# Eight transformer layers on one core: the attention gelu of half 0 placed ahead of half 1's second affine step on the scalar engine

## The reference: what is computed

```python
residual = x
Q = fmap(x @ Wq[i] + bq[i])          # fmap(t) = elu(t) + 1
K = fmap(x @ Wk[i] + bk[i])
value = x @ Wv[i] + bv[i]
KV = jnp.einsum('nsh,nsh->nh', K, value)
Ksum = jnp.sum(K, axis=1)
Z = 1.0 / (Q * Ksum[:, None, :] + EPS_ATTN)
V = Q * KV[:, None, :] * Z
attn_out = gelu(V @ Wo[i] + bo[i])
x = _ln(attn_out + residual, ln1_s[i], ln1_b[i])
residual = x
h = gelu(x @ W1[i] + b1[i])
ff_out = gelu(h @ W2[i] + b2[i])
x = _ln(ff_out + residual, ln2_s[i], ln2_b[i])
```

## Time and profile before

| | us |
|---|---|
| median of 3 runs | 715.82 |
| lowest and highest of the 3 | 714.5 and 719.45 |
| the profiled execution, its time | 718.21 |
| the profiled execution, its span | 716.4 |
| PE busy in the span | 633.6 (88%) |
| DVE busy | 432.8 (60%) |
| ACT busy | 318.1 (44%) |
| mean granted PE clock | 0.946 of full speed |

### The profile page before, as it was taken

One profiled execution on the slowest core, in us unless ns is written; L12 is line 12 of the kernel. 1 busy time (PEld: TensorE's weight loads), 2 busy tenths in 40 slices (PEclk: granted clock), 3 DMA queues, 4 the chain that ended last, 5 costly groups with the idle time before them and its releaser, 6 DMA issues.

```text
span 716.4 us, 9508 instructions
## 1 busy us (share of the span) xinstructions
PE 633.6 (88%) x3301; PEld 432.7 (60%) x3301; DVE 432.8 (60%) x1023; ACT 318.1 (44%) x504; POOL 114.4 (16%) x93
## 2 busy tenths in 40 slices
PE   9986899899999898888888898888876988999996
PEld 4755585787777364555555554545455866555595
DVE  5479503347758757666666666575765588643444
ACT  4035202234444556565555656574633434344341
POOL 0030130003230011110111111102032146200000
PEclk9599967989999999999999999999998999999997
DMA  3011388100000501000010101010000000000000
GB/s 86 25 44 46 95 255 175 29 1 1 0 1 1 146 1 44 2 21 25 0 44 0 44 0 44 0 44 1 0 1 0 1 1 0 1 0 1 0 1 30
DMA packets 43726, 21.79 MB, mean 30 GB/s; under 512 B 14627, under 2 KB 40799, under 8 KB 43692
## 3 DMA queue, kind: packets, MB, share of 16 engines
q1 hardware_dynamic: 43692, 21.33, 11.3%
HBM read 20.73 MB, written 0.52 MB: 30 GB/s over the span
## 4 chain that ended last, share of the span: by engine, by line
PE 44%; issue 29%; DVE 19%; POOL 5%; ACT 3%; POOLq 0%; DVEq 0%
PE ps L1515 6%; PE ps L1498 6%; POOL rstd L493 5%; PE ps L1702 5%; PE ps L1720 4%; PE ps L1249 3%; DVE zr L1053 2%; PE ps L1726 2%; DVE z L1012 2%; PE ps L1295 2%; PE ps L1376 2%; PE ps L1582 1%; PE ps L1389 1%; DVE xn L841 1%; PE ps L1416 1%
## 5 line engine op out<-in xcount | busy, mean ns | idle before, releaser
L493 POOL TENSOR_TENSOR rstd<-rv,minus_half 128x4 f32<-128x4 f32 x34 | 47.3, 1392 | 312.0 <-DVE rv L830 312.0
L660 ACT ACTIVATE zr<-ps 128x512 fp32r<-128x512 f32 x96 | 57.5, 599 | 80.0 <-PE ps L1498 76.0
L1053 DVE SCALAR_TENSOR_TENSOR zr<-ps,zr 128x512 fp32r<-128x512 f32 x96 | 63.7, 689 | 47.9 <-ACT zr L660 47.6
L1582 PE MATMUL ps<-cf,wl 128*128 128x512 f32 x128 | 68.5, 640 | 6.9 <-ACT cf L568 6.9
L1588 PEld LDWEIGHTS ps<-wl,z 128*128 128x128 f32 x512 | 64.0, 192 | 17.5 <-ACT z L722 8.7
L815 DVE TENSOR_TENSOR yt<-ps,z 128x512 f32<-128x512 f32 x32 | 22.1, 692 | 80.2 <-ACT z L727 42.4
L1588 PE MATMUL ps<-wl,z 128*128 128x128 f32 x512 | 68.4, 276 | 0.0
L1515 PE MATMUL ps<-zr 128*128 128x512 f32 x192 | 60.8, 398 | 7.8 <-DVE zr L1053 7.8
L1249 PE MATMUL ps<-filler 128*128 128x512 bf16 x246 | 62.9, 401 | 1.2 <-POOL filler L481 0.9
L1498 PE MATMUL ps<-zr 128*128 128x512 f32 x192 | 61.5, 402 | 1.4 <-DVE zr L994 1.4
L1206 DVE SCALAR_TENSOR_TENSOR z<-z,kc 128x512 f32<-128x512 f32 x48 | 34.6, 751 | 46.0 <-ACT z L775 44.2
(11 more groups left out here) (255 smaller groups left out, 1120.9 us busy)
## 6 DMA issues: line engine op xcount, KB each, us to landing
wl<-in_L_attn_W SPq DMA_DIRECT2D x16, 256.0 KB
big<-in_L_cond_weight SPq DMA_DIRECT2D x32, 64.0 KB, 1.8
arena<-in_L_cond_expert_wi SPq DMA_DIRECT2D x1, 1024.0 KB, 6.6
arena<-in_L_cond_expert_wo SPq DMA_DIRECT2D x4, 256.0 KB, 7.5
big<-in_L_ffn_q_w SPq DMA_DIRECT2D x2, 512.0 KB, 5.2
big<-in_L_ffn_k_w SPq DMA_DIRECT2D x2, 512.0 KB, 7.4
tree_v<-in_L_ffn_v_w SPq DMA_DIRECT2D x2, 512.0 KB, 7.4
arena<-in_L_cond_share_wi SPq DMA_DIRECT2D x1, 768.0 KB, 6.6
```

Source lines behind the costliest of these rows:

```text
L493: nc.gpsimd.tensor_tensor(rstd[:, half, :], rv[:, half, :], minus_half[:, :], ALU.pow).then_inc(S_["rstd"], 1)
L660: nc.scalar.activation(hidden_part(h, n, 0), ps[h][:, n % 2, :], ACT.Relu).then_inc(S_[k + "_hi"], 1)
L1053: V.scalar_tensor_tensor(hidden_part(h, n, 1), ps[h][:, n % 2, :], 0.0, hidden_part(h, n, 0), ALU.max, ALU.subtract).then_inc(S_[k + "_lo" ...
L1582: T.matmul(ps[h][:, FFN_BANK[c], :], wl[s][:, 4 * D + c * P:4 * D + (c + 1) * P], cf[:, h], start=True, stop=True).then_inc(S_["f_w1"], 1)
```

## The change

In ACT's `layer`, the call `gelu_o(l, 0)` moves from behind `affine(l - 1, 1, 1 - s, 1)` to ahead of it. In the first layer, which has no such affine step, nothing changes. No other engine's list changes.

```diff
             def layer(l, s, first=False):
                 feature_maps(l, 0, s)
                 ratio(l, 0)
+                gelu_o(l, 0)
                 if not first:
                     affine(l - 1, 1, 1 - s, 1)
-                gelu_o(l, 0)
                 feature_maps(l, 1, s)
                 affine(l, 0, s, 0)
                 ratio(l, 1)
```

## The result

| | before | after |
|---|---|---|
| median, four runs of each (us) | 717.06 (714.5 to 719.45) | 705.21 (703.01 to 707.69) |
| profiled execution, time and span | 718.21, 716.4 | 707.69, 705.8 |
| mean granted PE clock | 0.946 | 0.952 |

The ratio is 0.9843, with a 95% interval from 0.9812 to 0.9874: 1.6% faster. The prediction was 705.6 us and a span of 706.2. Two runs of one later kernel (the kernel before without fillers, 733.41 and 734.68 us) are over 1.5% slower than its fastest and enter no ratio.

A forecast was written before the change was run, and what follows sets the result against it. PE leads, and in each layer its wait for L841, behind the late gelu, ends last. 6.9 us from seven layers plus 3.3 from the clock make 10.2: 715.82 to 705.6 us, range 702.5 to 710.6.

The forecast's parts named there:

- The gelu's place: On ACT in layers 1 to 7: gelu L711 starts 1.11 us earlier, right behind attn_out; affine step L568 0.06 late.
- The chain behind it: DVE from L815 through half 1's queries L1092 to scaling L841 can move 1.11 us earlier; queries have 0.16 to spare.
- What is late next: PE's fillers ahead of the transposes then bound the layer; transposes end 0.98 us earlier per layer, between 0.82 and 1.11.
- The overlap of 0.16: PE's next instruction starts 0.16 us before the modelled end of the one before; without overlap the gain is 0.82.
- Seven layers: The change affects layers 1 to 7, each 0.98 us shorter: 6.9 us together, 5.7 to 7.8 by the ends.
- The clock: Two layers at 1.2 GHz instead of 2.4 cost 1.65 us each; both falls go, 3.3 us, between 0 and 5.0.
- the idle of 0.71 us: PE's wait for scaling L841 ahead of the layer's transposes, before both clock falls; the change takes it out.
- Its rival of more falls: Clock falls in more layers, 1.65 us each; six or seven hit layers lose, all seven give 717.1 us; chance 0.04.
- Its sign of no low clock up to 530 us: In the profile after, no low PE clock between 280 and 530 us; a layer of 37.7 us would refute the clock term.
- The parts that I took as unchanged: Time ahead of and behind the eight attention layers; the change sits only in the layers, about 236 to 535 us.
- The table load: ACT's load L687 runs after the affine step, 1.28 us from the trace; a skill's 2.66 would make the sum about 0.

The follow-up runs named there:

- the affine step was made 0.52 late: Changed kernel plus an unread 128x512 copy on ACT between gelu and affine step in layers 1 to 7; 711.79 us, ratio 0.9912 to before.
- seven fillers: Changed kernel with seven instead of four filler matmuls on PE ahead of the transposes of half 0's first norm; 711.27 us, ratio 0.9924 to before.
- one filler less: Changed kernel with three instead of four filler matmuls on PE ahead of the transposes of half 0's first norm; 707.33 us, ratio 0.9836 to before.
- before, seven fillers: Kernel before with seven instead of four filler matmuls on PE ahead of the transposes of half 0's first norm; 714.21 us, ratio 0.9949 to before.

## Why the prediction was right

**The number is closer than the reasoning.** The forecast change was 10.2 us, the medians differ by 11.85. The forecast started from a median of before of 715.82, which a fourth run moved to 717.06. The two errors nearly cancel, and that 705.6 lies 0.4 from 705.21 is luck; the terms are what can be checked.

**The gelu's place.** Forecast: the gelu 1.11 earlier, and the affine step 0.06 late. Shown: L815 waits 1.28 instead of 2.38, 1.10 less, and PE waits 0.05 longer for the affine step.

**The chain behind it.** Forecast: it moves as a whole, because the queries have 0.16 to spare. Shown: 4.55 from gelu to L841 as before, and, of the runs made, the queries waited only when the affine step was made 0.52 late.

**What is late next.** Forecast: PE's fillers, so that 0.98 of the 1.11 is kept. Shown: period 36.03 for 37.03, so 1.00; seven fillers cost all of their time and one filler less brought 0.11. Had I bound PE's next start by the modelled end of the fillers, it would have been 0.82. The overlap of 0.16, read from one pair of rows, decided that.

**Seven layers.** Forecast 6.9. Shown: the two profiles without a low clock in any layer give it directly: 295.31 (before, seven fillers) less 288.34 (after) is 6.97.

**The clock.** Forecast: both falls go, 3.3. Shown: 3.40 between before and before with seven fillers. The two terms must add up to the 10.37 of the layers' part, since both are taken over the same profile; the check on them is the single layers, where the periods differ by 1.00 and the two hit layers by 1.65 and 1.67 more. That the idle of 0.71 us matters is shown by filling it (ratio 0.9949, all of the interval below 1) and by taking all of its fillers away (1.0066, all of it above 1). Which layers are hit is not settled; nor is why, without fillers, 0.43 and 0.87 us of idle left seven layers untouched. In nine profiles with the gelu ahead everywhere, none of 63 layers with the new order had a low clock; of 25 with the old order (7 each in the two profiles of before and in that without fillers, 4 in that with the gelu ahead in three layers) seven had one, and of 7 with the old order and seven fillers none. The Trainium skill (TensorE: Matmul & The Clock Gate, "A second HAM failure mode: psum-queue depth-cycling") has short idles between groups of matmuls behind such falls, and the filled one agrees: no low clock in its seven layers. The prediction put every fall at 1.65 us, which was right for these two only: elsewhere one cost 1.5 or 3.2 to 3.3. Its rival of more falls has a slip: four more are 4 x 1.65 = 6.6, less than 6.9, so six hit layers would not have made the kernel slower. Its sign of no low clock up to 530 us missed the fall at 528.3, ahead of the last transposes.

**The parts that I took as unchanged** were not, by chance: 1.08 less ahead of the layers and 0.85 more behind. They nearly cancel. Such differences, and layer 0, where the clock may fall in either kernel, are of the size of the 5 us by which runs of one kernel spread; that they are that spread was not tested.

**The table load.** The row (1.28 and the next activation at once) was right and the 2.66 of the Trainium skill (ScalarE: Activation LUTs, "What ACT_TABLE_LOAD costs") would have been wrong here: L687 starts at 352.43, L696 at 353.73, 1.30 behind it. That section of the Trainium skill splits its figure into a load of about 1.28 us and a drain of about 1.38 us. The trace agrees with the first, 1.28, and shows no time for the second.

## What to carry to other kernels

On an engine that runs its list in order, put first what is ready first. Look at who posts the two semaphores: here PE posted the gelu's semaphore 0.43 us before the affine step's, and the reverse order cost 1.1 us on the longer path to save 0.06 on the shorter. Then ask what is late next, and by how much; of 1.1 us here PE's own list left 1.0.

Where the tensor engine idles for less than a microsecond at a time, look at the granted clock layer by layer before summing up waits: here a third of the gain in the layers was clock (3.4 of 10.4 us in the profiles), and three more unused matmuls per layer in the same gap bought about that third alone.

## What the hardware showed that I had not expected

- Fillers that nobody waits for are worth time: without four of them per layer the kernel before is 0.7% slower (0.3 to 1.1%) with no instruction held up, and with three more it is 0.5% faster.
- A fall of the clock costs 1.5 to 1.7 us or about twice that (3.2 to 3.3), for layers of the same work.
- While POOL casts and subtracts 128x1024 tiles behind the layers, DVE's two multiplications L841 take 3.72 us instead of 0.75, and PE's idle of 4.86 us there ends only with the first of them. No run took POOL's work away, so that it slows DVE is read from the times alone. The timeline of after:

```profile
527.03 1.03 POOL L514 CAST zr<-arena 128x1024 fp32r<-128x1024 f32 x1
527.10 3.72 DVE L841 TENSOR_TENSOR xn<-yt,rstd 128x256 f32<-128x256 f32 x2 [0.90 <-POOL rstd L493]
528.14 2.40 POOL L515 TENSOR_TENSOR arena_r<-arena,zr 128x1024 fp32r<-128x1024 f32 x1
```
